# Attention: value products three slots behind their unit, probability rings of three, value banks copied behind the high half

## The reference

```python
    xq, xk = _apply_rope(xq), _apply_rope(xk)          # 32 query heads, 8 key/value heads, 16 wide
    keys = jnp.repeat(xk, N_REP, axis=1)
    values = jnp.repeat(xv, N_REP, axis=1)
    scores = jnp.einsum('bhsd,bhtd->bhst', xq, keys) * scale
    scores = jnp.where(causal, scores, -jnp.inf)
    probs = jax.nn.softmax(scores, axis=-1)
    out = jnp.einsum('bhst,bhtd->bhsd', probs, values)
    out = out.transpose(0, 2, 1, 3).reshape(bs, seq, N_HEADS * HEAD_DIM)
    return out @ w_o
```

## Time and profile before

| | |
|---|---|
| median of 3 runs | 1827.2 us (1826.59 to 1828.6) |
| profiled execution, its own time | 1826.81 us |
| its span on the core | 1825.0 us |
| PE busy | 1660.2 us (91%) |
| PE weight loads busy | 1388.1 us (76%) |
| DVE busy | 1084.3 us (59%) |
| ACT busy | 802.9 us (44%) |
| POOL busy | 606.1 us (33%) |

### The profile page before, as it was taken

One profiled execution on the slowest core, in us unless ns is written; L12 is line 12 of the kernel. 1 busy time (PEld: TensorE's weight loads), 2 busy tenths in 40 slices (PEclk: granted clock), 3 DMA queues, 4 the chain that ended last, 5 costly groups with the idle time before them and its releaser, 6 DMA issues. The chain is left out here.

```text
span 1825.0 us, 26347 instructions
## 1 busy us (share of the span) xinstructions
PE 1660.2 (91%) x8965; PEld 1388.1 (76%) x8965; DVE 1084.3 (59%) x2298; ACT 802.9 (44%) x1723; POOL 606.1 (33%) x792
## 2 busy tenths in 40 slices
PE   5999995999999999999999999948989899899884
PEld 4899983888888888777877887837878778778773
DVE  7788854444466655674243323546777777767773
ACT  4675752222322231222222222217877777776760
POOL 5464542121111112442111113364244344444422
PEclk9999996999999999999999999969999999999997
DMA  3000002000111011321011102100000000000000
GB/s 127 26 24 13 1 1 70 28 24 19 30 39 34 26 29 34 125 73 50 21 30 38 33 29 81 52 24 1 1 7 7 13 1 12 13 1 13 13 7 19
DMA packets 32968, 54.27 MB, mean 30 GB/s; under 512 B 3840, under 2 KB 9120, under 8 KB 32832
## 3 DMA queue, kind: packets, MB, share of 16 engines
q1 hardware_dynamic: 32832, 52.55, 9.3%
HBM read 43.10 MB, written 9.44 MB: 29 GB/s over the span
## 5 line engine op out<-in xcount | busy, mean ns | idle before, releaser
L1196 POOL TENSOR_TENSOR m_a_lo<-m_prod,m_a_hi 128x512 fp32r<-128x512 f32 x100 | 134.4, 1344 | 642.0 <-ACT m_a_hi L1271 641.9
L1422 DVE TENSOR_TENSOR m_prod<-m_prod,m_ps 128x512 f32<-128x512 f32 x100 | 68.8, 688 | 389.3 <-ACT m_prod L1267 389.3
L1267 ACT ACTIVATE m_prod<-m_ps 128x512 f32<-128x512 f32 x100 | 59.7, 597 | 543.7 <-PE m_ps L116 543.7
L1898 ACT ACTIVATE t_p<-t_ps,t_nmax 128x128 f32<-128x128 f32 (+1 forms) x512 | 181.2, 425 | 70.1 <-DVE t_nmax L2019 69.3
L2019 DVE TENSOR_REDUCE t_nmax<-t_ps 128x2 f32<-128x512 f32 (+1 forms) x192 | 132.0, 688 | 79.4 <-PE t_ps L2095 42.2
L2025 DVE TENSOR_TENSOR t_pT_lo<-t_ps,t_pT_hi 128x512 fp32r<-128x512 f32 x192 | 131.3, 684 | 37.8 <-ACT t_pT_hi L1891 37.2
L1891 ACT ACTIVATE t_pT_hi<-t_ps 128x512 fp32r<-128x512 f32 x192 | 116.7, 608 | 53.5 <-PE t_ps L2102 53.0
L114 PE MATMUL m_ps<-m_hT_hi,m_w_hi 128*128 128x512 f32 x312 | 123.3, 395 | 0.6 <-DVE f_w_lo L1314 0.6
L116 PE MATMUL m_ps<-m_hT_hi,m_w_lo 128*128 128x512 f32 x312 | 123.4, 395 | 0.0
L115 PE MATMUL m_ps<-m_hT_lo,m_w_hi 128*128 128x512 f32 x312 | 123.1, 395 | 0.0
L2102 PE MATMUL t_ps<-consts,t_p 128*128 128x128 f32 x768 | 115.2, 273 | 1.9 <-ACT t_p L1898 1.9
(11 more groups left out here) (287 smaller groups left out, 4705.9 us busy)
## 6 DMA issues: line engine op xcount, KB each, us to landing
m_raw<-in_w_mlp SPq DMA_DIRECT2D x75, 256.0 KB, 2.8
a_xt<-in_x SPq DMA_DIRECT2D x8, 512.0 KB, 3.7
m_old<-in_x SPq DMA_DIRECT2D x16, 256.0 KB, 4.1
x_store<-stream SPq DMA_DIRECT2D x4, 1024.0 KB, 5.1
m_old<-x_store SPq DMA_DIRECT2D x16, 256.0 KB, 2.7
out<-t_yl SPq DMA_DIRECT2D x16, 256.0 KB, 2.0
m_raw<-in_w_attn SPq DMA_DIRECT2D x10, 256.0 KB, 2.8
a_att<-in_w_mixer SPq DMA_DIRECT2D x8, 256.0 KB, 2.8
```

Source lines behind the costliest of these rows:

```text
L1196: pool.tensor_tensor(a_lo[:, n % 2, :], prod[:, :], f(a_hi[:, n % 2, :]), ALU.subtract).then_inc(lo, 1)
L1422: dve.tensor_tensor(prod[:, :], prod[:, :], ps[:, U + TURN_AT["unit", n, 0] % 2, :], ALU.mult).then_inc(prodd, 1)
L1898: last = act.activation(p[:, u % 2, h * width:(h + 1) * width], ps[:, S + u % 2, h * width:(h + 1) * width], ACT.Exp, bias=nmax[:, u % 3, ...
```

## The change

`values(s - 2)` becomes `values(s - 3)`: in each slot PE multiplies the probabilities of the unit three slots back. The rings `t_pT_hi` and `t_pT_lo` get three buffers, and `high(u)` and `low(u)` wait for the value products of unit `u - 3`. On ACT `high(s - 1)` moves ahead of the `values_out` of the same slot. The slots of the `values_out` copies, the job table and all banks in PSUM stay as they are.

```diff
+PT_RING = 3
-        pT_hi = m.sb("t_pT_hi", [P, 2, 512], F32R)
-        pT_lo = m.sb("t_pT_lo", [P, 2, 512], F32R)
+        pT_hi = m.sb("t_pT_hi", [P, PT_RING, 512], F32R)
+        pT_lo = m.sb("t_pT_lo", [P, PT_RING, 512], F32R)
...
             def high(u):
                 act.wait_ge(tr, u + 1)
-                wait(act, pv, u - 1)
-                act.activation(pT_hi[:, u % 2, :], ps[:, T + u % 2, :], ACT.Copy).then_inc(ph, 1)
+                wait(act, pv, u + 1 - PT_RING)
+                act.activation(pT_hi[:, u % PT_RING, :], ps[:, T + u % 2, :], ACT.Copy).then_inc(ph, 1)
...
                 drain(s)
+                if 0 <= s - 1 < SLOTS:
+                    high(s - 1)
                 if n in (0, 2) and in_batch(b - 1):
                     values_out(2, n // 2, b - 1)
...
-                if 0 <= s - 1 < SLOTS:
-                    high(s - 1)
                 if 0 <= s + 1 < SLOTS:
                     exponentials(s + 1)
...
             def low(u):
                 dve.wait_ge(ph, u + 1)
-                wait(dve, pv, u - 1)
-                dve.tensor_tensor(pT_lo[:, u % 2, :], ps[:, T + u % 2, :], f(pT_hi[:, u % 2, :]), ALU.subtract).then_inc(pl, 1)
+                wait(dve, pv, u + 1 - PT_RING)
+                dve.tensor_tensor(pT_lo[:, u % PT_RING, :], ps[:, T + u % 2, :], f(pT_hi[:, u % PT_RING, :]), ALU.subtract).then_inc(pl, 1)
...
                 if 0 <= s + 1 < SLOTS:
                     scores(s + 1)
-                if 0 <= s - 2 < SLOTS:
-                    values(s - 2)
+                if 0 <= s - PT_RING < SLOTS:
+                    values(s - PT_RING)
```

More of the change, by code:

```diff
@@ L2116, in values @@
                 if r == 0:
-                    pe.matmul(ps[:, OT, :], v(0), pT_hi[:, u % 2, :], start=fresh, stop=False)
-                    mm = pe.matmul(ps[:, OT, :], v(0), pT_lo[:, u % 2, :], start=False, stop=final)
+                    pe.matmul(ps[:, OT, :], v(0), pT_hi[:, u % PT_RING, :], start=fresh, stop=False)
+                    mm = pe.matmul(ps[:, OT, :], v(0), pT_lo[:, u % PT_RING, :], start=False, stop=final)
                 else:
                     out = ps[:, OT + 1, (r - 1) * SEQ:r * SEQ].rearrange("p (h n) -> p h n", h=2)
-                    of = lambda part, t: part[:, u % 2, :].rearrange("p (h t n) -> p h t n", h=2, t=2)[:, :, t, :]
+                    of = lambda part, t: part[:, u % PT_RING, :].rearrange("p (h t n) -> p h t n", h=2, t=2)[:, :, t, :]
                     for t in range(2):
```

## The result

| | before | after |
|---|---|---|
| median of 20 runs each | 1827.07 us (1824.4 to 1829.22) | 1824.01 us (1818.94 to 1827.63) |
| profiled execution, its own time | 1826.81 us | 1825.46 us |
| span | 1825.0 us | 1823.7 us |
| PE, DVE, ACT, POOL busy | 1660.2, 1084.3, 802.9, 606.1 us | 1657.1, 1083.6, 803.8, 606.8 us |

The ratio is 0.9983, with a 95% interval of 0.9976 to 0.999: faster by 3.1 us (1.8 to 4.4). The forecast was 1822.9.

What follows compares the result with a forecast made beforehand. PE was taken to lead, DVE and ACT close behind. Head 1.0, rest of first batch 1.1, slot 3 1.6 and last batch 0.6 sum to 4.3 us, giving 1822.9 us; own range 1816 to 1825, overall 1813 to 1829.

Steps and rivals of the forecast that it cites:

- What all products wait: All value products' waits for the low half: 34.2 us in 51 cases, less 0.15 each, 26.5 us removable.
- Slot 3: Middle batches, slot 3: the 0.27 us stall is saved for good, 1.6 us over six batches.
- Slots 15 to 18: Middle batches: nothing gained; a 13.5 us chain on ACT and DVE holds, and PE's key and query waits grow by 1.35.
- Slot 1: Middle batches, slot 1: nothing gained; PE arrives 0.53 us earlier and waits 0.53 longer for the key copy.
- Head: First batch, slot 2 loses its value product, so its transposes come earlier: 1.0 us saved, between 0.47 and 1.4.
- Rest of the first batch: First batch after its head: stalls of slots 12 to 18 give nothing, slot 19's stall of 1.11 us gives 1.1.
- Last batch: Last batch: DVE and ACT serve each other with or without PE; 0.6 us saved, slots 14 to 18 nothing.
- `high` ahead of `values_out`: nothing: ACT's new order, six times a batch: no gain; in slot 9 ACT may lose 0.3 us before the exponentials.
- A: Rival, chance 0.10: rings of two make the bubbles, so all 26.5 us of stalls go, 1800.7 us.
- B: Rival, chance 0.12: value bank copies hold ACT, 6 us lost in the first and last batch, 1832.2 us on the median.
- Its other sign: Sign of B: transposes that wait for exponentials, beside value bank copies on ACT waiting for PE over 0.3 us each.
- C: Rival, chance 0.15: every stall reappears at the transposes or next bank; only 1.0 us at the head stays, 1826.2 us.

Runs made afterwards that it cites:

- e4: The changed kernel with the four transposes of slot 16 done five times over in each batch; 1826.2 us against 1828.88 before the change, one run.
- e5: The changed kernel with the four transposes of slot 12 done five times over in each batch; 1836.35 us against 1828.88 before the change, one run.
- e6: The changed kernel without one half key copy on ACT in slot 17, from the second batch on; 1813.61 us against 1828.88 before the change, one run.
- e6b: The changed kernel without one half key copy on ACT in slot 6, from the second batch on; 1822.22 us against 1828.88 before the change, one run.
- e8_jobs: The changed kernel with the jobs of slots 13 to 17 spread differently over the same slots; 1820.73 us, ratio 0.9966 to the kernel before the change.

## Why the prediction held, and where it did not

**What all products wait: the size was off, not the reading.** After a stall the next product starts 0.22 us later, not 0.12. The timeline before, slots 12 and 16, beside the earlier trace rows:

```profile
1400.45 0.28 PE L2124 MATMUL t_ps<-t_pT_lo,t_v 128*128 128x256 f32 x1
...
1411.76 0.28 PE L2124 MATMUL t_ps<-t_pT_lo,t_v 128*128 128x256 f32 x1
```

1411.54 to 1411.76 against 1400.34 to 1400.45. I calibrated on the start of the first product and left out that it moves on late. With it the stall of slot 16 is 0.67 us where the weight load says 0.71, that is 0.04 off, not 0.15. In the trace before, all 33 products of 256 columns with idle time ahead of them are followed after 0.22 to 0.23 us, so the 51 stalls are 34.2 - 51 x 0.04 = 32.2 us and not 26.5. The sum didn't suffer much, since only slot 3 and pieces of the outer batches were kept in it.

**Slot 3: kept, and larger.** Predicted 0.27 a batch; measured 3.46 us for the slot before and 3.09 after in five of the six middle batches, so 0.37. By the corrected calibration 0.42 - 0.04 = 0.38. In the first middle batch the slot gets only 0.08 shorter (3.61 to 3.53). That is 5 x 0.37 + 0.08 = 1.93 us in all, and the six batches gave 1.48: the first middle batch gives back 0.44 in its slot 1, part of what the first batch had won. So the 1.6 that I had forecast came out near 1.48 with some luck, by two misses that nearly cancel.

**Slots 15 to 18: nothing, as said.** Their sum is 2.64 + 2.80 + 3.03 + 3.35 = 11.82 us before and 2.66 + 2.33 + 3.50 + 3.35 = 11.84 after. The same place as the earlier trace rows in the timeline after:

```profile
1484.59 0.84 ACT L1900 ACTIVATE t_p<-t_ps,t_nmax 128x256 f32<-128x256 f32 x2 [1.11 <-DVE t_nmax L2021]
1485.32 1.19 ACT L1853 ACTIVATE t_kT<-t_ps 64x512 fp32r<-64x512 f32 x2
...
1486.55 0.42 PEld L2171 LDWEIGHTS t_ps<-consts,t_stacks 128*128 128x128 f32 x4 [1.67 <-ACT t_kT L1853]
1487.02 0.59 ACT L1893 ACTIVATE t_pT_hi<-t_ps 128x512 fp32r<-128x512 f32 x1
...
1489.93 0.63 PE L2158 MATMUL t_ps<-consts,t_xf 128*128 128x128 f32 x4 [1.48 <-DVE t_xf L1945]
```

The exponentials wait 1.11 us for the maximum as they did, and from them to the turned tile it takes 5.34 us (1484.59 to 1489.93), where it took 5.35. Only PE's waits in front grew. I expected 4.3 us of them a batch and found 4.8, the same under-sizing of the stalls. Four experiments carry it: 1.75 us more on PE is free here (e4) and not in slot 12 (e5), 0.6 us less on ACT counts in full (e6) and not in slot 6 (e6b).

**Slot 1: nothing, as said.** The key wait ahead of the tile at 1439.33 is 0.80 us where it was 0.17.

```profile
1439.33 0.66 PE L2158 MATMUL t_ps<-consts,t_xf 128*128 128x128 f32 x4 [0.80 <-ACT t_kT L1853]
```

**Head: 1.0 predicted, 0.80 measured.** Slot 2 lost its products, and its transposes are held by the low half:

```profile
1244.60 0.69 DVE L2027 TENSOR_TENSOR t_pT_lo<-t_ps,t_pT_hi 128x512 fp32r<-128x512 f32 x1 [0.76 <-ACT t_pT_hi L1893]
...
1245.44 0.63 PE L2104 MATMUL t_ps<-consts,t_p 128*128 128x128 f32 x4 [0.54 <-DVE t_pT_lo L2027]
```

From slot 1's transposes to these it takes 2.05 us; before it took 2.85. **Rest of the first batch: 1.1 predicted, 1.05 measured** (1.85 - 0.80). It came in pieces, not in slot 19 alone: the lead was 1.23 us by slot 12, 0.92 by slot 17 and 1.90 by slot 19. **Last batch: 0.6 predicted, 0.47 measured.** Both terms were followed, and which waits gave their 1.52 of the 3.80 us no experiment shows; with the head's 0.80 the outer batches hold 2.3 of it. One slip in the range: a third of the outer batches' 12.7 us would end at 1820.4, not at the 1816 that I wrote.

**"`high` ahead of `values_out`: nothing" is the step that was wrong, though the sum hides it.** I costed the two edits apart. Taken alone the order is worth little (0.5 us), as I said. But the later products make the copy wait for a product of PE's same slot, and I let this fall on the exponentials only, in the new order, without asking what it would do in the old one. It holds ACT for 41.2 us in the layer with the old order and for 8.2 with the new one. 3.07 of the 3.80 us hang on the order: 0.73 in the first batch, 1.44 in the middle ones, 0.90 in the last. The sum came out right since its terms assumed the combination; the credit for them was put in the wrong edit. Slots 2 and 3 after, on ACT and DVE, show how little the copy now delays:

```profile
1441.10 0.60 ACT L1893 ACTIVATE t_pT_hi<-t_ps 128x512 fp32r<-128x512 f32 x1
...
1441.58 0.62 ACT L1888 ACTIVATE t_oT<-t_ps 128x512 f32<-128x512 f32 x1
...
1442.11 1.14 ACT L1900 ACTIVATE t_p<-t_ps,t_nmax 128x128 f32<-128x128 f32 x4
1442.59 0.68 DVE L2027 TENSOR_TENSOR t_pT_lo<-t_ps,t_pT_hi 128x512 fp32r<-128x512 f32 x1
```

High half, copy and exponentials follow each other without idle time. The kernel with the copy first had copy 1439.53, high half 1440.02, exponentials 1440.49, the same three in the other order, so in slot 2 itself the copy costs the high half one operation and no wait; the holds stand in slots 0, 9, 11 and 20.

**The rivals.** A fell with the first result, and its ground with the rings of three alone; the bubbles that repeat were not a want of buffers (the Trainium skill, "Perfetto Trace Analysis", Identifying Performance Opportunities, says that they can be; here 34.2 us of waits stood with two buffers and with three). B's mechanism is real, but it belongs to the old order: there it costs 0.73 + 0.90 = 1.6 us in the outer batches, where B had 6, and 1.4 in the middle ones, where B had none. I gave it a chance for the order that avoids it. Its other sign, transposes that wait for exponentials, is there in the new order, 10.1 us in 13 cases, and the copy's hold is 8.2 / 28 = 0.29 us each, just under the 0.3 that I had named (0.35 in slot 11). PE arrives earlier at these transposes, so such waits come with a gain as well as with a loss: the sign was badly chosen. C did not come: slot 3 kept its gain, and the first batch most of its.

**What stays open.** The measured 3.1 us has an interval of 1.8 to 4.4, the layer's 3.80 comes from one profile on either side. A fall of the granted clock moved the unchanged layers by 1.57 us at one place; why it falls at one place in one profile and not in another was not tried, nor whether it makes up all of the difference. Which wait of slots 1 to 3 carries each tenth of the 0.24 us that the order is worth there is shown only in part. What the order costs is measured in all batches, where the outer batches' gain of 2.3 us stands in detail only for the head.

## What to carry to other kernels

Ask of a stall on the leading engine what is late next at the same place: PE gained only where nothing else waited behind it (slots 2 and 3 above all), and nothing in the four slots that ACT and DVE set. When a step is moved later, look at every reader of its result on the in-order engines, and at what stands behind that reader: the copy of the result has to move too, and only as far as its own reader allows. Then shorten the chain itself: moving two half copies a batch to the other engine gave 9.2 us, more than twice what removing 34 us of waits gave. And before a small difference is put down to an edit, look at the granted clock in the stretch: it made e8_jobs look like an idea that didn't work.

## What the runs showed of the hardware

- A product that starts after a stall is followed by the next one 0.22 us later, where 0.12 is usual for 256 columns (33 cases before). PE's busy time drops when stalls go: 484.8 us after against 490.4 before over 1237 to 1780, with no fewer instructions (3248 and 3235 records).
- Sixteen more transposes of 128 columns in float32 take 1.75 us, 0.11 us each (e4_pe_load_16).
- TensorE's granted clock fell to half for a few us at places that differ between profiles of the same work, behind a wait of PE that the other profile has too (2.13 and 1.80 us in one case, 2.17 and 2.17 in e8_jobs): one fall cost 1.57 us (4.15 against 2.58 us, mean clock 0.59 against 1.00). The work that the change doesn't touch took 1284.7 to 1292.3 us in 14 profiles, a spread of twice what this change is worth. The 20 runs of the changed kernel alone lie 8.7 us apart, and the shortest, 1818.94 us, has the highest mean granted clock, 0.976 (the others 0.969 to 0.972). One kernel had a shorter layer (534.43 against 535.16) and a longer median (1829.53 against 1827.27).
